# Two fused transformer layers on one core: early weight loads behind the last maxima, another order of the first front, and eight bits before the next maximum

## The chip, the cores and the metric

The kernel runs on one core of a Trainium2 chip. The metric is the device time of one execution in microseconds (us).

## The reference

The input x is (4, 1024, 512) in fp32. Two layers are computed one after the other. The first, "layer 0", is a style-modulated layer norm, an attention with 16 heads of 32 columns, a projection and a second norm:

```python
h = _sln(hidden, w, ...)                      # gamma * ln(hidden) + beta
energy = jnp.einsum('bhqd,bhkd->bhqk', q, k)
att = jax.nn.softmax(energy, axis=-1) / D ** 0.5
h1 = out @ Wp.T + bp + hidden
return _sln(h1, w, ...) + h1
```

The second, "layer 1", does the same kind of attention and a feed-forward block of 2048 columns, with weights of three values and activations of eight bits:

```python
def act_quant(x):
    s = 127.0 / jnp.clip(jnp.max(jnp.abs(x), axis=-1, keepdims=True), EPS)
    return jnp.clip(jnp.round(x * s), -128, 127) / s
xn = adaln(x, c, g1, w_ada1, b_ada1)          # rmsnorm(x) * g * (1 + scale) + shift
x = x + bitlinear(attention(bitlinear(xn, w_qkv, b_qkv)), w_proj, b_proj)
xn = adaln(x, c, g2, w_ada2, b_ada2)
h = jax.nn.gelu(bitlinear(xn, w_fc1, b_fc1), approximate=False)
x = x + bitlinear(h, w_fc2, b_fc2)
```

## The kernel before

The program is written out by hand for the five engines: TensorE (PE), VectorE (DVE), ScalarE (ACT), GpSimd (POOL) and SyncE (SP), which issues the DMAs. Semaphores order them. There are three blocks: `layer0`, `layer1a` (layer 1 up to the attention's projection) and `layer1b` (the feed-forward part). Between two blocks all engines meet.

**Attention.** The class `Attention` serves both layers. One batch has 16 rows (heads). For each row, `max_chunk` (L369) makes 16 chunks of scores whose maxima DVE reduces (L500), two rows ahead of use; these maxima become a row of 8 KB ("row of maxima") that ACT copies out of PSUM (`m_row`, L465) and that SP moves into the last two partitions of q by `load_m` (L295). Only then do the real scores start (`scores`, L383): the first score of a row waits for that transfer. ACT takes the exponential (L461), POOL adds probabilities up three by three (`sums`, L338 and L343), and PE multiplies them with the values and the sums with ones (L401) and folds the result (L408). SP's order is written in `run_sp`: at step k it issues the six pieces of q and k of row k + 3 (`load`, L290), or, at k = 13, when no such row is left, calls `late()`; then it waits for the maxima of row k + 1 and issues `load_m`.

In the last batch of either layer `late()` also holds the loads for the block to come. In `layer0` these are the q/k/v and projection weights of layer 1 (L761, L762). In `layer1a` they are fc1, a quarter of x, the modulation, two biases and fc2 (L1536), six transfers. At k = 13 all of them stand on SP's queue ahead of the `load_m` of rows 14 and 15.

**Fronts.** Ahead of each batch's attention in `layer1a` stands a front: four transposes ("X"), sixteen products of q and k ("QK", each a half of 128 columns) and eight of v ("V"). `products` (L1484 to L1501) writes out their order; the last 14 of them each have two chunks of maxima behind them (a "part", "prelude"). For batch 0 nothing else runs beside the front; for batches 1 to 3 the front is spread over the attention before it and joined with its tail. A QK product is scaled by DVE (L1776), ACT writes its rounded high half (`high`, L1702), and DVE (`low`, L1786; the first eight) or POOL (L1599, after ACT has made the whole value at L1705; the last eight) writes the low half. A V product is scaled by ACT (L1691), and POOL adds the bias (L1582). `load` of row 0 waits for four high and four low halves; ACT's first exponential waits for all sixteen. The value bias lies in memory that the last high half overwrites, so `high` waits for all bias adds at m = KC + 3. The order for batch 0 before is

```python
order = X + both(QK[:EARLY], V) + QK[EARLY:]      # EARLY = 8; both() takes from the two lists in turn
chunks = order[-att.PRELUDE:]                     # PRELUDE = 14
```

and POOL does all eight bias adds, then the eight low halves.

**The last block.** `layer1b` has 32 tiles of 128 tokens. Each engine has a list of stages with offsets; at step n it runs stage f for tile n + offset. For DVE these are the maximum of h (offset 0), the de-quantization of fc1 (`hidden`, L2083, offset 2), the maximum of x (`maximum(0)`, L2050, offset 5), the eight bits of x (`x_bits`, L2074, offset 4), the eight bits of h (`h_bits`, L2089, offset 0) and the residual. PE transposes x (L1950), does fc1 (L1959), transposes h (L1968) and does fc2 (L1978). ACT scales x (L2001), rounds it (L2005), copies transposes (L2009, L2024) and does Gelu. The block opens on ACT with a dummy Sqrt (L1986), the Sqrt of the mean squares (L1988) and a dummy Gelu (L1989), so that the function tables are loaded there.

Of the kernel before, what the change touches and what calls it, by code (L numbers as in the profile page):

```python
# [142 lines left out]
class Attention:  # L143
# [158 lines left out]
    def run_sp(self, sp, b, late, extra=None, ready=None):  # L302
# [4 lines left out]
        def head(i, k, N, ok, steps):  # L307
# [8 lines left out]
            if ok(k + 1):  # L316
                self.load_m(sp, N + 1, (k + 1) % NJ)
        self.loop(b, head)
# [234 lines left out]
def layer0(nc, ins, mod, x_in, x_out, ss1, ident, ps):  # L553
# [4 lines left out]
    with ctx:  # L558
# [141 lines left out]
        with nc.Block() as block:  # L700
            @block.sync
            def _(sp):
# [46 lines left out]
                def batch(b, last):  # L749
                    def late():  # L750
# [7 lines left out]
                        sp.dma_start(bp, rows(ins["bp"], P)).then_inc(s_late, 16)  # L758
                        if last:
                            sp.wait_ge(s_wout, 16 * (2 + done(2) - done(1)))  # L760
                            sp.dma_start(next_w[:, :, :], wq["qkv"]).then_inc(s_next, 16)  # L761
                            sp.dma_start(next_wp[:, :, :], wq["proj"]).then_inc(s_next, 16)  # L762
# [19 lines left out]
                    att.run_sp(sp, b, late, ready=ready)  # L782
# [620 lines left out]
def layer1a(nc, ins, mod, wq, dws, x_in, x_out, ss1, ss2, ident, identb, ps):  # L1403
# [5 lines left out]
    with ctx:  # L1409
# [71 lines left out]
        def products(nxt, tail):  # L1481
# [4 lines left out]
            if not tail:  # L1486
                order = X + both(QK[:EARLY], V) + QK[EARLY:]
# [27 lines left out]
        with nc.Block() as block:  # L1515
            @block.sync
            def _(sp):
# [6 lines left out]
                def attend(b, last):  # L1524
                    def late_load():
                        sp.dma_start(bp, rows(ins["b_proj"], P)).then_inc(s_late, 16)
                        if not last:
                            sp.dma_start(bv, rows(ins["b_v"], P)).then_inc(s_bv, 16)
                            return
                        sp.wait_ge(KINDS["V"][1], TT * B)  # L1530
                        sp.wait_ge(s_store, 16 * TT + 16)
# [11 lines left out]
                    att.run_sp(sp, b, late_load, extra)  # L1543
# [6 lines left out]
                    if not last:  # L1550
                        att.first_loads(sp, b + 1, (2,))

# [19 lines left out]
            def _(pool):  # L1572
# [4 lines left out]
                def work(order, nxt, tail):  # L1577
# [5 lines left out]
                    if nxt is not None:  # L1583
                        biases(range(TT if tail is None else LEAD))
                        if tail is not None:
                            pool.wait_ge(s_q, TT * (tail + 1))
                            biases(range(LEAD, TT))
                    if tail is not None:
                        pool.wait_ge(s_late, 16 * (tail + 1))
                        for t in range(TT):  # L1590
                            if t % 2 == 0:
                                pool.wait_ge(s_res[t // 2], 16 * (tail + 1))
                            pool.tensor_tensor(xres[:, t, :], xres[:, t, :], bp, ALU.add).then_inc(s_xb, 1)
                    if nxt is None:
                        return
                    for v in range(EARLY, UN):
                        pool.wait_ge(s_whole, (UN - EARLY) * nxt + v - EARLY + 1)
                        hi, lo = parts(v)
                        pool.tensor_tensor(lo, qf(v), hi.bitcast(FP32), ALU.subtract).then_inc(s_lo, 1)  # L1599
                pool.sem_inc(s_xb, 1)  # L1600
# [4 lines left out]
            def _(pe):  # L1605
# [46 lines left out]
                def work(order, nxt, tail):  # L1652
                    if nxt is not None and tail is not None:
                        pe.wait_ge(s_qf, UN * nxt + EARLY)
                    for kind, n, bank, before, part in order:
# [3 lines left out]
                        if part is not None:  # L1659
                            if part == 0:  # L1660
# [7 lines left out]
            def _(act):  # L1668
# [24 lines left out]
                def high(n, nxt, tail):  # L1693
# [4 lines left out]
                    if m == KC + 3:  # L1698
                        act.wait_ge(s_val, TT * (nxt + 1))
                        if tail is not None:  # L1700
                            act.wait_ge(s_xb, TT * nxt + 1)
# [142 lines left out]
def layer1b(nc, ins, mod, wq, dws, x_in, out, ss2, identb, ps):  # L1844
# [11 lines left out]
    with ctx:  # L1856
# [23 lines left out]
        one, s_one = sb("one", [P, 2], FP32), sem("one_ok")  # L1880
# [27 lines left out]
        with nc.Block() as block:  # L1908
# [76 lines left out]
            def _(act):  # L1985
                act.activation(one[:, 0:1], identb[:, 0:1], ACT.Sqrt).then_inc(s_one, 1)  # L1986
# [175 lines left out]
```

## Time and profile before

| | |
|---|---|
| median of 3 runs | 2920.75 us (2918.14 to 2922.14) |
| profiled execution, its own time | 2920.18 us |
| its span, first to last instruction | 2918.3 us |
| busy in the span | PE 92%, DVE 76%, POOL 69%, ACT 63%, weight loads 52% |
| mean granted clock of PE | 0.970 |

The profiled execution's time is its span and 1.9 us around it. A line of a timeline has the start in us from the span's start, the duration, the engine, the line of the kernel, the operation, what is written and read, how many instructions are merged, and in square brackets the idle time before and who ended it.

### The profile page before, as it was taken

To read this page: it belongs to the slowest core of one execution; us is meant where nothing else is said; L and a number is where in the kernel's file an instruction comes from. 1 tells how busy PE (TensorE), PEld (TensorE's weight loads), DVE (VectorE), ACT (ScalarE), POOL (GpSimd) and SP (SyncE) were. 2 spreads that over 40 slices of the span, in tenths; PEclk is the share of its full clock that TensorE was granted. 3 is DMA by queue.
4 is the path that set the end of the run, shared out by engine and by line. 5 is a ranking of instruction groups with operands and counts; after the bars stand their busy time and mean duration, and the time that the engine had idled before them with its cause. 6 is when DMAs were issued, how large, how long until landed. Compare 5 with 4: busy or idle time off the path is not lost. (4 is left out here: it accounts for less than half of the span.)

```text
span 2918.3 us, 62297 instructions
## 1 busy us (share of the span) xinstructions
PE 2686.3 (92%) x22313; PEld 1514.9 (52%) x22313; DVE 2216.5 (76%) x4450; ACT 1838.4 (63%) x3314; POOL 2022.7 (69%) x1703
## 2 busy tenths in 40 slices
PE   7899999999999989999669998998999899958998
PEld 6655466554765547555235554554555455424444
DVE  4777678776887768878667768777887777649997
ACT  3366654665566654666346677667666766548887
POOL 0299824996269951899539997997899799854441
PEclk9999999999999999999879999999999999979999
DMA  6122343223432424223123214322232232440000
GB/s 217 39 62 56 123 128 120 56 63 135 138 91 57 128 77 152 70 56 117 51 69 74 60 31 113 81 64 70 74 78 53 62 85 62 144 166 23 29 29 36
DMA packets 102183, 243.57 MB, mean 83 GB/s; under 512 B 18812, under 2 KB 25092, under 8 KB 101000
## 3 DMA queue, kind: packets, MB, share of 16 engines
q1 hardware_dynamic: 100104, 233.49, 28.2%
q0 software_dynamic: 1792, 6.33, 0.6%
q8 instruction: 172, 2.82, 0.4%
q14 instruction: 115, 0.94, 0.1%
HBM read 99.15 MB, written 38.88 MB: 47 GB/s over the span
## 5 line engine op out<-in xcount | busy, mean ns | idle before, releaser
L500 DVE TENSOR_REDUCE a_mxs<-ps 128x1 f32<-128x512 f32 x2048 | 1269.5, 682 | 269.0 <-PE ps L369 266.6
L461 ACT ACTIVATE a_p<-ps 128x512 f32<-128x512 f32 x2048 | 1043.7, 605 | 209.4 <-PE ps L383 200.0
L338 POOL TENSOR_TENSOR a_sum<-a_p 128x512 f32<-128x512 f32 x768 | 989.0, 1294 | 95.8 <-PE ps L401 76.2
L369 PE MATMUL ps<-a_k,a_q 96*128 96x512 f32 x2048 | 858.6, 425 | 34.4 <-DVE a_mxs L500 27.0
L383 PE MATMUL ps<-a_q,a_k 98*128 98x512 f32 x2048 | 812.0, 420 | 23.6 <-ACT a_p L461 11.3
L343 POOL TENSOR_TENSOR a_sum<-a_sum,a_p 128x512 f32<-128x512 f32 x512 | 664.6, 1298 | 40.2
L401 PE MATMUL ps<-a_sum,a_unit 128*32 128x512 f32 x1536 | 657.8, 599 | 17.3 <-POOL a_sum L343 14.6
L401 PE MATMUL ps<-a_p,a_vx 128*32 128x512 f32 x4096 | 665.0, 599 | 1.0 <-DVE tok L519 0.8
L369 PEld LDWEIGHTS ps<-a_k,a_q 96*128 96x128 f32 x2048 | 390.2, 191 | 270.5 <-DVE a_mxs L500 113.0
L383 PEld LDWEIGHTS ps<-a_q,a_k 98*128 98x128 f32 x2048 | 385.0, 189 | 261.5 <-ACT a_p L461 158.9
L470 ACT ACTIVATE a_ots<-ps 128x512 f32<-128x512 f32 x256 | 152.8, 598 | 423.1 <-PE ps L401 422.1
L401 PEld LDWEIGHTS ps<-a_sum,a_unit 128*32 128x32 f32 x1536 | 134.7, 110 | 184.1 <-issue 147.8
L401 PEld LDWEIGHTS ps<-a_p,a_vx 128*32 128x32 f32 x4096 | 166.9, 110 | 109.3 <-issue 74.0
L517 DVE RECIPROCAL a_rec<-ps 128x4 f32<-128x4 f32 x256 | 45.1, 176 | 167.4 <-PE ps L408 167.4
L1934 POOL TENSOR_TENSOR c_tk<-c_tk,b_next_mod 128x512 f32<-128x512 f32 x32 | 40.7, 1271 | 153.7 <-ACT c_tk L2001 153.7
L408 PEld LDWEIGHTS ps<-a_fold,a_ots 128*32 128x32 f32 x8192 | 99.0, 111 | 90.0 <-issue 85.9
L1978 PE MATMUL ps<-b_next_w,c_hT 128*128 128x512 bf16 x512 | 120.5, 379 | 22.1 <-ACT c_hT L2024 22.1
L846 POOL TENSOR_TENSOR kh<-kh,qh 128x512 f32<-128x512 f32 x32 | 43.1, 1346 | 129.1 <-ACT a_p L1080 128.7
L1959 PE MATMUL ps<-b_next_w,c_xqT 128*128 128x512 bf16 x512 | 120.0, 389 | 4.9 <-ACT c_xqT L2009 2.6
L408 PE MATMUL ps<-a_fold,a_ots 128*32 128x33 f32 x8192 | 119.7, 198 | 2.0 <-ACT a_ots L470 2.0
L966 PE MATMUL ps<-qh,ql 128*128 128x512 f32 x256 | 110.8, 593 | 3.3 <-ACT ql L1074 3.3
L1582 POOL TENSOR_TENSOR xv<-xv,kh 128x512 f32<-128x512 f32 x32 | 40.1, 1271 | 81.5 <-ACT xv L1691 81.5
(240 smaller groups left out, 3190.8 us busy)
## 6 DMA issues: line engine op xcount, KB each, us to landing
a_q<-qh SPq DMA_DIRECT2D x256, 128.0 KB, 2.3
a_k<-kh SPq DMA_DIRECT2D x256, 128.0 KB, 2.4
a_q<-ql SPq DMA_DIRECT2D x128, 128.0 KB, 2.4
a_k<-kl SPq DMA_DIRECT2D x128, 128.0 KB, 2.4
x<-a_p SPq DMA_DIRECT2D x64, 256.0 KB, 2.1
a_p<-in_w_fc SPq DMA_DIRECT2D x12, 1024.0 KB, 8.0
kl<-in_x SPq DMA_DIRECT2D x4, 2048.0 KB, 9.5
kh<-in_x SPq DMA_DIRECT2D x4, 2048.0 KB, 14.4
```

The source lines that it names most:

```text
L338: pair = pool.tensor_tensor(tile, self.key_tile(u, kt), self.key_tile(u, kt + 1), ALU.add)
L343: pool.tensor_tensor(tile, tile, self.key_tile(u, kt + 2), ALU.add).then_inc(self.s_sum, 1)
L369: pe.matmul(self.mx[self.mx_ring[at]], self.q[j][0:96, t * P:(t + 1) * P], self.k[j][0:96, half * HALF:(half + 1) * HALF], start=True, sto ...
L383: pe.matmul(self.st[self.st_ring[at]], self.k[j][0:98, kt * P:(kt + 1) * P], self.q[j][0:98, u * HALF:(u + 1) * HALF], start=True, stop=Tr ...
L401: mm = pe.matmul(self.ot[half % 2][HD * c:HD * (c + 1), :], weights, tile, start=r == rounds[0], stop=r == rounds[-1])
L408: mm = pe.matmul(self.ot[u][HD * c:HD * (c + 1), t * (HD + 1):(t + 1) * (HD + 1)], self.ots[:, u, t * P + HD * c:t * P + HD * (c + 1)], se ...
L461: act.activation(self.key_tile(u, kt), self.st[self.st_ring[CHUNKS * k + n]], ACT.Exp, scale=self.scale).then_inc(self.s_exp, 1)
L470: act.activation(self.ots[:, u, :], self.ot[u], ACT.Copy).then_inc(self.s_ots, 1)
L500: dve.reduce_max(self.mxs[:, k % 2, c:c + 1], self.mx[self.mx_ring[CHUNKS * k + c]], axis=AX.X).then_inc(self.s_mxr, 1)
L966: mm = pe.matmul(ps[:, t, :], oT[:, k, t * P:(t + 1) * P], wp[:, k, :], start=k == 0, stop=k == KC - 1)
L1959: mm = pe.matmul(f1[:, j, :], xqT[:, r % 2, k, :], w1[:, k, j * HALF:(j + 1) * HALF], start=k == 0, stop=k == KC - 1)
L1978: mm = pe.matmul(f2, hT[:, r % 2, k, :], w2[:, k, :], start=k == 0, stop=k == FC - 1)
```

## The change

It has five parts. `run_sp` takes a function `after()` and calls it behind the `load_m` of row 15. The loads for the block to come move from `late()` there, in both layers; in `layer1a` x and the modulation now go first, and fc2 goes behind the four residual loads that follow the attention. The order of batch 0's front in `layer1a` has the first eight QK products alone, then V and the last eight QK products in turn; POOL takes bias adds and low halves in turn, and `high` waits for the bias adds at its last call alone. The dummy Sqrt moves from the head of `layer1b` to the head of ACT's last work in `layer1a`. In `layer1b`, DVE's list has `x_bits` ahead of `maximum(0)`.

```diff
@@ Attention.run_sp
             if ok(k + 1):
                 self.load_m(sp, N + 1, (k + 1) % NJ)
+                if not ok(k + 2):
+                    after()
@@ layer0, SP
+                    def after():
                         if last:
                             sp.wait_ge(s_wout, 16 * (2 + done(2) - done(1)))
                             sp.dma_start(next_w[:, :, :], wq["qkv"]).then_inc(s_next, 16)
@@ layer1a, products
-                order = X + both(QK[:EARLY], V) + QK[EARLY:]
+                order = X + QK[:EARLY] + both(V, QK[EARLY:])
@@ layer1a, SP
-                        for dst, src in ((next_w1[:, :, :], wq["fc1"]), (next_x[:, 0:TT, :], x_out[0:T, :].rearrange("(t p) d -> p t d", p=P)),
-                                         (next_mod[:, 0, :, :].rearrange("p i d -> p (i d)"), rows(Pending.mods[2][0, :, :].rearrange("i d -> (i d)"), P)),
-                                         (next_b1[:, :], rows(ins["b_fc1"], P)), (next_b2[:, :], rows(ins["b_fc2"], P)),
-                                         (next_w2[:, :, :], wq["fc2"])):
-                            sp.dma_start(dst, src).then_inc(s_next, 16)
+                    def after():
+                        if last:
+                            sp.wait_ge(KINDS["V"][1], TT * B)
+                            sp.wait_ge(s_store, 16 * TT + 16)
+                            for dst, src in ((next_x[:, 0:TT, :], x_out[0:T, :].rearrange("(t p) d -> p t d", p=P)),
...
+                                             (next_w1[:, :, :], wq["fc1"]), (next_b1[:, :], rows(ins["b_fc1"], P)),
+                                             (next_b2[:, :], rows(ins["b_fc2"], P))):
+                                sp.dma_start(dst, src).then_inc(s_next, 16)
...
                     if not last:
                         att.first_loads(sp, b + 1, (2,))
+                    else:
+                        sp.dma_start(next_w2[:, :, :], wq["fc2"]).then_inc(s_next, 16)
@@ layer1a, POOL
-                        biases(range(TT if tail is None else LEAD))
...
+                    if tail is None:
+                        for t in range(TT):
+                            biases((t,))
+                            rest(EARLY + t)
+                        return
@@ layer1a, PE
-                            if part == 0:
+                            if part == 0 and tail is not None:
                                 pe.wait_ge(s_vs, TT * nxt + EARLY_V)
@@ layer1a, ACT, high
-                    if m == KC + 3:
+                    if n == UN - 2 and tail is not None:
+                        act.wait_ge(s_xb, TT * nxt + 1)
+                    if n == UN - 1:
                         act.wait_ge(s_val, TT * (nxt + 1))
-                        if tail is not None:
-                            act.wait_ge(s_xb, TT * nxt + 1)
@@ layer1a, ACT, work
+                    if nxt is None:
+                        act.wait_ge(att.s_one, 1)
+                        act.activation(att.one[:, :], ident[:, 0:1], ACT.Sqrt).then_inc(att.s_one, 1)
@@ layer1b, ACT
-                act.activation(one[:, 0:1], identb[:, 0:1], ACT.Sqrt).then_inc(s_one, 1)
                 act.wait_ge(s_ms, 1)
                 act.activation(rs[:, :], ms[:, :], ACT.Sqrt).then_inc(s_sd, 1)
@@ layer1b, DVE
-                            (0, factor(1)), (5, maximum(0)), (4, x_bits), (5, clipped(0)), (0, h_bits), (5, inverse(0)),
+                            (0, factor(1)), (4, x_bits), (5, maximum(0)), (5, clipped(0)), (0, h_bits), (5, inverse(0)),
```

## Rows read from the trace of the kernel before

**Rows 1.** Waits of PE over the span: us in total, times, longest us

```profile
PE ps L383 <- DMA a_q<-a_mrow: 8.2, 4, 6.3
```

**Rows 2.** Timeline of SP, last batch of layer 1a

```profile
2515.37 0.38 SPq L1536 DMA_DIRECT2D b_next_w<-wq_fc  x1
...
2528.38 22.08 SPq L295 DMA_DIRECT2D a_q<-a_mrow  x2
```

**Rows 3.** Timeline of PE, last batch of layer 1a

```profile
2531.70 0.50 PE L369 MATMUL ps<-a_k,a_q 96*128 96x512 f32 x1
...
2539.22 0.76 PE L383 MATMUL ps<-a_q,a_k 98*128 98x512 f32 x1 [6.31 <-DMA a_q<-a_mrow]
...
2543.76 0.95 PE L401 MATMUL ps<-a_sum,a_unit 128*32 128x512 f32 x1
```

**Rows 4.** Timeline of PE, last batch of layer 0, the same instructions

```profile
1367.47 0.50 PE L369 MATMUL ps<-a_k,a_q 96*128 96x512 f32 x1
...
1371.29 0.62 PE L401 MATMUL ps<-a_sum,a_unit 128*32 128x512 f32 x1
```

**Rows 5.** Timeline of PE, first front of layer 1a

```profile
1480.79 1.91 PE L1628 MATMUL ps<-a_next_w,b_xqT 128*128 128x512 bf16 x4
...
1497.21 1.19 PE L369 MATMUL ps<-a_k,a_q 96*128 96x512 f32 x2 [6.58 <-issue]
...
1528.14 0.80 PE L383 MATMUL ps<-a_q,a_k 98*128 98x512 f32 x1 [1.72 <-ACT a_p L461]
```

**Rows 6.** Timeline of ACT, last tail of layer 1a and start of layer 1b

```profile
2579.11 5.01 ACT L1675 ACTIVATE tok<-tok,b_am 128x512 f32<-128x512 f32 x8 [5.61 <-DVE b_am L1753]
...
2604.14 1.28 ACT L1986 ACT_TABLE_LOAD   x1 [2.57 <-PEq L110]
...
2605.54 0.21 ACT L1988 ACTIVATE c_rs<-c_ms 128x32 f32<-128x32 f32 x1
...
2616.51 0.71 ACT L2005 ACTIVATE c_tk<-c_tk,c_am 128x512 f32<-128x512 f32 x1
```

**Rows 7.** Waits of PE, last two rows of layer 0 (1361.1 to 1403)

```profile
PE ps L401 <- POOL a_sum L343: 4.2, 3, 1.5
```

**Rows 8.** DMA issues of the page: count, KB each, median us to landing

```profile
b_next_w<-wq_fc SPq DMA_DIRECT2D x2, 2048.0 KB, 13.4
```

**Rows 9.** Timeline of DVE, first front of layer 1a

```profile
1489.94 1.57 DVE L1786 SCALAR_TENSOR_TENSOR kl<-ql,b_bqk,kh 128x512 fp32r<-128x512 f32 x1
...
1503.37 0.74 DVE L1786 SCALAR_TENSOR_TENSOR ql<-qh,b_bqk 128x512 fp32r<-128x512 f32 x1
...
1523.93 0.68 DVE L1776 TENSOR_TENSOR a_p<-ps,b_dqr 128x512 f32<-128x512 f32 x1
1524.52 3.07 DVE L500 TENSOR_REDUCE a_mxs<-ps 128x1 f32<-128x512 f32 x5
```

**Rows 10.** Timeline of SP, first front of layer 1a

```profile
1491.59 1.20 SPq L290 DMA_DIRECT2D a_q<-qh  x2
```

**Rows 11.** Timeline of POOL, first front of layer 1a

```profile
1505.23 1.27 POOL L1582 TENSOR_TENSOR xv<-xv,kh 128x512 f32<-128x512 f32 x1 [3.02 <-ACT xv L1691]
```

**Rows 12.** Busy time by window: us; PE, PEld, DVE, ACT, POOL; clock, DMA share, GB/s

```profile
1497.20:1503.30 6.10, 6.08 (x14) 2.79 (x14) 3.11 (x5) 0.69 (x1) 1.26 (x1) 0.50 0.92 207
1503.40:1526.00 22.60, 18.64 (x73) 8.68 (x73) 22.46 (x42) 14.30 (x21) 11.45 (x9) 1.00 0.10 22
```

**Rows 13.** Timeline of ACT, first exponentials of layer 1a

```profile
1527.49 2.08 ACT L461 ACTIVATE a_p<-ps 128x512 f32<-128x512 f32 x4 [1.37 <-POOL kl L1599]
```

**Rows 14.** Timeline of DVE, start of layer 1b

```profile
2604.18 0.18 DVE L2029 TENSOR_SCALAR c_ms<-ss 128x32 f32<-128x32 f32 x1 [3.37 <-PEq L110]
...
2614.38 0.69 DVE L2050 TENSOR_REDUCE c_am<-c_tk 128x1 f32<-128x512 f32 x1 [2.60 <-POOL c_tk L1938]
2614.98 0.87 DVE L2074 TENSOR_SCALAR c_xq<-c_tk 128x512 bf16<-128x512 f32 x1
```

**Rows 15.** Timeline of DVE, one tile in the loop of layer 1b

```profile
2762.34 1.23 DVE L2089 TENSOR_SCALAR c_hq<-c_h 128x2048 bf16<-128x2048 f32 x1 [0.17 <-ACT c_h L2019]
```

More of the change, by code:

```diff
@@ L300, in first_loads, with run_sp @@
             self.load(sp, b, H * b + j, 0, j)
-    def run_sp(self, sp, b, late, extra=None, ready=None):
+    def run_sp(self, sp, b, late, after, extra=None, ready=None):
         if ready:
@@ L781, in batch @@
                     att.load_m(sp, H * b, 0)
-                    att.run_sp(sp, b, late, ready=ready)
+                    att.run_sp(sp, b, late, after, ready=ready)
                     sp.wait_ge(att.s_pv, att.ROUNDS * H // 2 * (b + 1) + att.PV_CREDIT)
@@ L1542, in extra @@
                             front(b + 1)
-                    att.run_sp(sp, b, late_load, extra)
+                    att.run_sp(sp, b, late_load, after, extra)
                     if not last:
@@ L1582, in biases, with rest @@
                             pool.tensor_tensor(xv[:, t, :], xv[:, t, :], bv, ALU.add).then_inc(s_val, 1)
-                    if nxt is not None:
-                        biases(range(TT if tail is None else LEAD))
-                        if tail is not None:
[L1586 to L1596, printed above, removed]
+                    def rest(v):
                         pool.wait_ge(s_whole, (UN - EARLY) * nxt + v - EARLY + 1)
@@ L1599, in work @@
                         pool.tensor_tensor(lo, qf(v), hi.bitcast(FP32), ALU.subtract).then_inc(s_lo, 1)
+                    if tail is None:
[3 more added lines that the diff above has]
+                        return
+                    if nxt is not None:
+                        biases(range(LEAD))
+                        pool.wait_ge(s_q, TT * (tail + 1))
+                        biases(range(LEAD, TT))
+                    pool.wait_ge(s_late, 16 * (tail + 1))
+                    for t in range(TT):
+                        if t % 2 == 0:
+                            pool.wait_ge(s_res[t // 2], 16 * (tail + 1))
+                        pool.tensor_tensor(xres[:, t, :], xres[:, t, :], bp, ALU.add).then_inc(s_xb, 1)
+                    if nxt is not None:
+                        for v in range(EARLY, UN):
+                            rest(v)
                 pool.sem_inc(s_xb, 1)
@@ L1697, in high @@
                     act.wait_ge(s_qf, UN * nxt + n + 1)
-                    if m == KC + 3:
+                    if n == UN - 2 and tail is not None:
+                        act.wait_ge(s_xb, TT * nxt + 1)
+                    if n == UN - 1:
                         act.wait_ge(s_val, TT * (nxt + 1))
-                        if tail is not None:
-                            act.wait_ge(s_xb, TT * nxt + 1)
                     act.activation(parts(n)[0], qf(n), ACT.Identity, bias=bqk[:, m:m + 1]).then_inc(s_hi, 1)
@@ L1878, in layer1b @@
         col = lambda i, j, n: am[:, i, j, bass.ds(n, 1)]
-        one, s_one = sb("one", [P, 2], FP32), sem("one_ok")
+        one, s_one = sb("one", [P, 1], FP32), sem("one_ok")
         s_wsc = sem("wsc_ok")
@@ L1985, in _ @@
             def _(act):
-                act.activation(one[:, 0:1], identb[:, 0:1], ACT.Sqrt).then_inc(s_one, 1)
                 act.wait_ge(s_ms, 1)
                 act.activation(rs[:, :], ms[:, :], ACT.Sqrt).then_inc(s_sd, 1)
-                act.activation(one[:, 1:2], identb[:, 0:1], ACT.Gelu).then_inc(s_one, 1)
+                act.activation(one[:, :], identb[:, 0:1], ACT.Gelu).then_inc(s_one, 1)
                 act.sem_inc(s_xtc, 1)
```

5 lines of the change are left out of this document (2 added, 3 removed).

## The prediction

> **What bounds the kernel now.** I began with the page's busy times (the table above): TensorE is by far the busiest engine, so time comes back only where it stands still or runs at its lower clock. Next I read whom TensorE waited for [rows 1]. The entry that matters is 8.2 us in four waits for the transfer of the row of maxima, of which 6.3 us are a single one. Then I laid the timelines of all engines side by side around the three places that the diff touches.
>
> **Place 1, the early loads of the last batch of layer 1a.** SP issues the loads for the last block from 2515.37 on, and the 8 KB transfer of row 14's maxima only at 2528.38, behind them [rows 2]. TensorE stands still for 6.31 us until that transfer lands, and the matmuls behind it take until 2543.76 to reach the next group [rows 3]. Layer 0's last batch runs the same rows, and there TensorE doesn't wait at this point [rows 4].
>
> **Place 2, the first front of layer 1a.** TensorE stands still for 6.58 us before the first maxima at 1497.21 and for another 1.72 us behind the first scores, at 1528.14 [rows 5].
>
> **Place 3, the start of the last block.** Its first function table is loaded at 2604.14 with nothing else to do [rows 6].
>
> **Part by part.**
>
> *Loads behind the last row of maxima, layer 1a.* From the L369 matmul ahead of row 14's scores to the next L401 group takes 2543.76 - 2531.70 = 12.06 us [rows 3]; the same stretch in layer 0 takes 1371.29 - 1367.47 = 3.82 us [rows 4]. Without the queue the difference goes: **8.2 us**, the wait and the slower restart behind it together. At the upper end I put 8.5. The lower end is set by POOL's sums: in layer 0's last two rows TensorE waits 4.2 us for them [rows 7], and a TensorE that is no longer held up might meet that wait here, which leaves 4.0. I take 8.2, since in layer 0 VectorE adds a bias beside POOL in those rows and in layer 1a it doesn't. The moved loads hang on a wait of SP that both kernels satisfy long before. SP issues x, the modulation, fc1 and two biases after row 15's transfer, near 2542 (2528.38 + 22.08 [rows 2] - 8.2), and fc2 behind four residual loads, before the tail's first rounding, which is now at 2579.11 [rows 6], so by 2571. The transfers of fc1 and fc2 took 13.4 us to land [rows 8], so the last lands by 2584, ahead of the block that reads them, which opens near 2596 (2604.14 - 8.2). Behind them on SP stand only the output stores, which follow the tail. Cost: nothing, as long as those 12 us are there.
>
> *The same in layer 0.* TensorE shows no wait at that transfer [rows 4], so **0**. The bound from both sides is 0.3 us, the spacing of one score. The two weights move by some 20 us and are read 100 us later.
>
> *The order of the first front.* Row 0's pieces of q and k are loaded when four products have their high and low halves. The fourth low half starts at 1489.94 and takes 1.57 us [rows 9]; SP issues the first load at 1491.59 [rows 10]; TensorE's first maxima follow at 1497.21 [rows 5]. In the new order no value product stands between the first eight q/k products, and no value bias runs on POOL yet, so I take 0.74 us for a low half (the row at 1503.37, where POOL stands still: its next add, at 1505.23, follows 3.02 us of idling [rows 11]) instead of 1.57. The second product, now a q/k one, ends at 1480.79 + 1.91 = 1482.70 [rows 5]. Behind it VectorE has four scalings, 0.59 apart (1523.93 to 1524.52), and four low halves, 0.66 apart (1503.37 to the next row) [rows 9]: 1482.8 + 2.4 + 2.7 = 1487.9. Loads and first maxima are **3.6 us** earlier. The other gain lies behind them. Now all eight low halves and nine scalings precede the first maxima, where five low halves and six scalings did: 3 x 0.66 + 3 x 0.59 = **3.8 us** of VectorE work leave the stretch behind, in which VectorE sets the pace: from 1503.4 to 1526.0 it is busy 22.46 of 22.60 us, with TensorE at a granted clock of 1.00 and busy 18.64 [rows 12]. Against this stands a new wait. The last high half must not overwrite the value bias before POOL's eighth bias add, and POOL now does that add only after the seventh "rest"; each takes 1.27 us [rows 11]. Counting ACT's and POOL's queues from the last two products, the high half starts 1.0 to 1.1 us later than its scaling allows. ACT's exponentials wait for POOL's last rest (1527.49) [rows 13], and TensorE behind them (1528.14). Queued behind the waiting high half are only its own second half and the exponentials, so that is the whole price. Sum 3.6 + 3.8 - 1.0 = **6.4 us**. Lower end 3.6 (the loads alone); upper end 7.4, without POOL's part. In the joint rounds, where one batch's tail runs with the next one's front, the two high halves wait for the same POOL adds as before, in POOL's order: 0.
>
> *The Sqrt table.* The load (1.28 us) and its dummy go to the head of ACT's last work in layer 1a, where ACT stands still for 5.61 us [rows 6]: free there. If that cover were gone it would cost 1.5. In the last block the Sqrt starts at 2605.54; its input leaves VectorE at 2604.18 + 0.18 [rows 6, 14], so it can start near 2604.45: **1.1 us**. Ends: 0, and 1.4, the whole distance from 2604.14. The Trainium skill ("ScalarE: Activation LUTs", What ACT_TABLE_LOAD costs) puts a switch at about 1.28 us for the load and 1.38 us more to drain, so by it the sum would come to 18.1 and the time to 2902.1; the trace doesn't agree, for the Sqrt starts 0.12 us behind the load's end with the dummy in between.
>
> *Eight bits ahead of the next maximum.* Tile 0's eight bits came behind the maximum of tile 1, for which VectorE had stood idle 2.60 us until 2614.38; they ran at 2614.98 for 0.87 us [rows 14]. This looks like 2.6 us, but isn't: ACT copies tile 0's transposes only behind the rounding of tile 1 (2616.51) [rows 6], which needs tile 1's own maximum. With the eight bits out of the way, clip and inverse follow the maximum directly, and the rounding starts near 2615.5: **1.0 us**. Ends: 0 and 2.6. In the steady loop the maximum's result no longer has the eight bits as cover before its clip, yet the next operation, the eight bits of h, already waits 0.17 us for ACT there [rows 15]: cost 0. Ends: no gain, since TensorE's transposes of x aren't what it waits for there, and the loss of rival 4; I stay near the first, as only the latency of one result is exposed.
>
> **Sum:** 8.2 + 6.4 + 1.1 + 1.0 = 16.7 us, off the profiled execution's 2920.2: 2903.5. That execution lies 0.6 below the median of the runs, 2920.75; I give **2904.0**.
>
> **Rivals.**
> 1. *POOL takes over from the transfer.* The four-microsecond wait of layer 0 [rows 7] appears in layer 1a too: the first term is 4.0, the sum 12.5, the time 2908. For it: the last rows end on POOL sums in both layers. Against: VectorE's bias adds are absent. 10%.
> 2. *The prelude stays at TensorE's lower clock.* After the stop TensorE's granted clock is 0.50 (1.2 of 2.4 GHz) for 6.1 us, in which it does 14 matmuls [rows 12]; a part has six (four of a product, two of maxima), so it takes 2.6 us there. The later ones are paced by VectorE, with two reductions of 0.61 (3.07 / 5 [rows 9]) and every second time a scaling: 1.5 us. Were the last eleven slow too, 11 x 1.1 = 12.1 us would come back: the sum is 4.6, the time 2916. Against: TensorE will stand still for about 2.7 instead of 6.58 us. 7%.
> 3. *The table load comes back.* The last block opens with a load of its own, so that term is 0 and the sum 15.6: 2905. The Trainium skill ("ScalarE activation tables: per-element evaluation and per-set limits", Table sets in the compiler and the runtime) says that the table loads are placed per block. The trace leaves it open: in it every change of block is also a change of table. 8%.
> 4. *VectorE becomes the bound of the last block.* In each of 32 tiles the maximum (0.69 us [rows 14]) is no longer covered and h's eight bits come that much later: 32 x 0.69 = 22.1 us lost, the sum is -5.4, the time 2926, slower than before. It decides from the point where the clip comes more than the 0.17 us of slack late in every tile and TensorE's transposes of h wait for it. Against: only a result's latency is exposed, not the maximum. 4%.
> 5. *The change does nothing in place 1*, because the transfer itself was slow and not the loads ahead of it: 2912. Only four of these transfers were waited for at all, the other three for 1.9 us together [rows 1], so I put this within the rest.
>
> **How the numbers follow.** Forecast 68%, rivals 10, 7, 8 and 4%, rest 3%. About 0.2% (5.8 us) is what a measurement of this kernel can tell from no change. The forecast, rivals 1 to 3 and a third of the rest are faster: 94%. Rival 4 lies at the edge between same and slower, so I split it and what is left of the rest: 4% same, 2% slower. The range goes down to 2898, where the upper ends of all terms lie (8.5 + 7.4 + 1.4 + 2.6 = 19.9) with 2 us to spare for a clock that rises earlier, and up to 2911, which holds rival 1 and any one term at its lower end. Rivals 2, 4 and 5 stay outside.
>
> **What would show it.** TensorE's wait on the maxima's transfer without the 6.3 us; the first load of row 0 near 1488 and the first exponential near 1521 instead of 1527.5; no table load between the two layers' blocks except that of Gelu, and the first fc1 matmul some 2 us sooner after the block's start; an unchanged period of a tile in the loop. Wrong would be: a POOL wait of over 3 us in layer 1a's last two rows, products 1.7 us apart until the prelude's end, or a longer tile period.

## The result, and the profile after

The changed kernel took 2897.76 us in the median of 4 runs (2896.73 to 2900.11), the kernel before beside it 2919.44 (2917.23 to 2922.14): a ratio of 0.9926, interval 0.9909 to 0.9944, or 21.7 us less. The forecast was 2904.0, so the direction is right and the median lies 0.24 us under the range's low end. Two further comparisons of the same two kernels, told below, give 17.3 and 17.5 us. The profiled execution took 2898.03 us with a span of 2896.3.

Lines of the changed kernel stand 2 to 17 lower in the file than those of before. TensorE's waits over the whole span, the row that answers to [rows 1]:

```profile
PE ps L385 <- DMA a_q<-a_mrow: 2.8, 4, 1.3
```

The 6.3 us wait is gone. In place 1, SP now issues row 14's and row 15's transfers ahead of every load (timelines of SP and of TensorE, last batch of layer 1a, for [rows 2] and [rows 3]):

```profile
2515.86 13.50 SPq L295 DMA_DIRECT2D a_q<-a_mrow  x2
2529.47 0.40 SPq L1543 DMA_DIRECT2D b_next_x<-x  x1
```

```profile
2519.19 0.50 PE L371 MATMUL ps<-a_k,a_q 96*128 96x512 f32 x1
2519.53 0.40 PE L385 MATMUL ps<-a_q,a_k 98*128 98x512 f32 x1
...
2523.01 0.62 PE L403 MATMUL ps<-a_sum,a_unit 128*32 128x512 f32 x1
...
2549.40 1.03 PE L403 MATMUL ps<-a_sum,a_unit 128*32 128x512 f32 x1 [1.51 <-POOL a_sum L345]
...
2550.22 1.06 PE L403 MATMUL ps<-a_sum,a_unit 128*32 128x512 f32 x1
```

The stretch of 12.06 us is 2523.01 - 2519.19 = 3.82 us, to the hundredth what layer 0 had [rows 4]. But at the attention's end the groups behind the wait for POOL follow each other 0.82 us apart (2549.40 to 2550.22), where they stood 0.43 us apart until then: the granted clock is 0.50 from 2549.40 to 2552.00, so TensorE runs at 1.2 GHz there.

The first front, for [rows 5, 9 to 13]: SP, TensorE, VectorE, POOL and ACT in turn.

```profile
1482.04 1.20 SPq L290 DMA_DIRECT2D a_q<-qh  x2
```

```profile
1487.62 1.22 PE L371 MATMUL ps<-a_k,a_q 96*128 96x512 f32 x2 [2.69 <-DMA a_k<-kh]
...
1515.99 0.80 PE L385 MATMUL ps<-a_q,a_k 98*128 98x512 f32 x1 [2.26 <-ACT a_p L463]
```

```profile
1481.23 0.74 DVE L1803 SCALAR_TENSOR_TENSOR kl<-ql,b_bqk,kh 128x512 fp32r<-128x512 f32 x1
...
1490.61 0.69 DVE L1793 TENSOR_TENSOR a_p<-ps,b_dqr 128x512 f32<-128x512 f32 x1 [0.87 <-PE ps L1642]
1491.22 1.28 DVE L502 TENSOR_REDUCE a_mxs<-ps 128x1 f32<-128x512 f32 x2
1493.62 1.29 DVE L502 TENSOR_REDUCE a_mxs<-ps 128x1 f32<-128x512 f32 x2 [1.12 <-PE ps L371]
```

```profile
1511.13 1.26 POOL L1591 TENSOR_TENSOR xv<-xv,kh 128x512 f32<-128x512 f32 x1
1514.04 1.26 POOL L1596 TENSOR_TENSOR kl<-a_p,kh 128x512 fp32r<-128x512 f32 x1 [1.65 <-ACT a_p L1719]
```

```profile
1512.48 0.73 ACT L1716 ACTIVATE kh<-a_p,b_bqk 128x512 fp32r<-128x512 f32 x1 [1.94 <-POOL xv L1591]
...
1515.34 2.08 ACT L463 ACTIVATE a_p<-ps 128x512 f32<-128x512 f32 x4 [1.37 <-POOL kl L1596]
```

The first load starts 0.07 us behind the fourth low half (1481.23 + 0.74), and the low halves take 0.74 us as forecast. The new wait of the last high half for POOL's bias is there, 1.94 us long. This execution is 6.0 us ahead when layer 0 ends (see below); with these set back, the first load lies at 1488.05 and the first exponential at 1521.35, where 1488 and 1521 were forecast. In the windows view (columns as in [rows 12]) the first maxima run at 1.2 GHz, after that VectorE again sets the pace:

```profile
1487.60:1493.80 6.20, 5.93 (x13) 2.79 (x14) 3.35 (x6) 2.89 (x5) 3.90 (x4) 0.50 0.92 204
1493.80:1512.00 18.20, 16.54 (x67) 7.75 (x67) 17.95 (x34) 10.34 (x17) 13.74 (x12) 0.99 0.06 14
```

Place 3, for [rows 6, 14, 15]: ACT, then VectorE at the last block's start and in its loop.

```profile
2553.38 1.28 ACT L1725 ACT_TABLE_LOAD   x1
2554.67 0.20 ACT L1725 ACTIVATE a_one<-ident 128x1 f32<-128x1 f32 x1
...
2585.86 0.23 ACT L2004 ACTIVATE c_rs<-c_ms 128x32 f32<-128x32 f32 x1 [2.76 <-DVE c_ms L2045]
2586.11 1.28 ACT L2005 ACT_TABLE_LOAD   x1
```

```profile
2585.64 0.18 DVE L2045 TENSOR_SCALAR c_ms<-ss 128x32 f32<-128x32 f32 x1 [3.30 <-PEq L110]
...
2592.79 0.83 DVE L2090 TENSOR_SCALAR c_xq<-c_tk 128x512 bf16<-128x512 f32 x1 [0.68 <-ACT c_tk L2021]
2594.78 0.69 DVE L2066 TENSOR_REDUCE c_am<-c_tk 128x1 f32<-128x512 f32 x1 [1.16 <-POOL c_tk L1955]
...
2634.10 0.15 DVE L2073 TENSOR_SCALAR c_am<-c_am  x1 [0.15 <-DVE c_am L2066]
2634.18 1.23 DVE L2105 TENSOR_SCALAR c_hq<-c_h 128x2048 bf16<-128x2048 f32 x1
```

The Sqrt stands 0.22 us behind its input's start (1.36 before), with no load of its own; the only load left in the block is Gelu's. Tile 0's bits come 2 us ahead of tile 1's maximum. In the loop only a result's latency of 0.15 us is exposed, and the eight bits of h no longer wait.

**Where the 22 us lie.** I took the start of ACT's copy of each row of maxima (line 465 before, 467 after) as a mark in both traces and subtracted. The changed kernel is ahead by 1.1 us at the first mark, and by 6.0 us at the last one of layer 0 (1376.77 against 1370.76), where the change has done nothing yet but hold back loads in layer 0's last rows. Layer 1a's first front adds 6.3, place 1 adds 8.6 (21.09 at the last mark of layer 1a), the rest of layer 1a loses 2.6, and the last block's start gains 3.2 again. So the change's own steps make about 16 us of this pair, and 6 us came from somewhere else. Of these, 1.1 stand at the first mark, some 1.4 in layer 0's front ahead of its second batch and 3.3 in the one ahead of its fourth. What follows asks from where.

### The profile page after: what moved, and what is told of

Read it like the earlier page. It is cut to its first block and busy times, and to the rows that moved or that the text cites. A ratio compares the mean times of both kernels' runs of the same rounds, so it can differ in the third digit from the quotient of the medians.

```text
span 2896.3 us, 62255 instructions
## 1 busy us (share of the span) xinstructions
PE 2671.8 (92%) x22259; PEld 1509.2 (52%) x22313; DVE 2214.3 (76%) x4450; ACT 1836.7 (63%) x3314; POOL 2020.8 (70%) x1703
```

## The experiments

Each kernel was timed beside the kernel before. Besides the times I read the same stretches from each kernel's one profiled execution, as differences of starts in its timelines; they tell single steps apart better than a median. **L0** is a front of layer 0, from row 15's mark of its third batch to row 0's of the fourth; **front** goes from layer 0's last mark to layer 1a's mark of row 1; **place 1** from its mark of row 14 to that of row 15 in the last batch; **end** from there to VectorE's last write of the attention's result; **tail** to c_ms, the mean squares that VectorE writes first in the last block; **block** to the first fc2 matmul. All in us.

| kernel | L0 | front | place 1 | end | tail | block |
|---|---|---|---|---|---|---|
| before | 138.96 | 157.82 | 21.46 | 24.74 | 29.88 | 38.21 |
| e1, loads alone | 135.49 | 157.92 | 12.87 | 25.78 | 31.53 | 37.76 |
| e2, front alone | 135.61 | 149.36 | 20.90 | 24.76 | 30.25 | 37.75 |
| e3, block alone | 135.87 | 159.40 | 21.25 | 24.66 | 31.07 | 34.92 |
| e4, layer 0 alone | 137.09 | 159.31 | 21.32 | 24.68 | 30.36 | 38.03 |
| after | 135.69 | 151.51 | 12.88 | 25.69 | 31.48 | 34.98 |
| e5, the same | 137.22 | 150.36 | 12.86 | 25.73 | 31.48 | 35.01 |
| e14, the same | 138.66 | 149.42 | 12.88 | 24.71 | 30.06 | 35.53 |
| e6, without block | 135.68 | 149.35 | 12.88 | 24.66 | 31.37 | 37.71 |
| e8, idle products | 138.70 | 149.34 | 12.89 | 24.68 | 30.44 | 34.15 |
| e9, V first | 135.91 | 148.40 | 12.88 | 25.70 | 31.45 | 35.01 |
| e12, before + idle | 138.86 | 158.01 | 21.38 | 24.70 | 29.73 | 36.03 |
| e11, e1 + idle | 135.91 | 159.33 | 12.89 | 25.72 | 29.93 | 36.01 |
| e10, e8 + e9 | 135.68 | 148.79 | 12.88 | 24.70 | 30.48 | 32.50 |
| e13, e10 + front idle | 135.74 | 148.31 | 12.87 | 25.75 | 30.19 | 32.50 |

### The parts alone

**e1**, layer 1a's loads behind the last row of maxima, layer 0 in its old order:

```diff
-                    att.run_sp(sp, b, late, ready=ready)
+                    att.run_sp(sp, b, late, lambda: None, ready=ready)
...
-                    att.run_sp(sp, b, late_load, extra)
+                    att.run_sp(sp, b, late_load, after, extra)
```

> Only the loads of the last block are moved behind the last row of maxima (layer 1a; layer 0 keeps its order). My theory (the parts add up as the steps of the prediction say; the 6 us by which the changed kernel is ahead in layer 0's fronts is how the clock fell in that execution, not the change): the first product over a row of maxima goes from 2531.70 us to some 8.4 us earlier, the end of the attention and the tail give back 2.5 us as in the changed kernel's trace (products at the lower clock), so 5.5 to 6.5 us faster in all, and layer 0's fronts end within 2 us of the kernel before. Rival A (giving back belongs to the other parts): 8.2 to 8.6 us faster. Rival B (this part also speeds up layer 0): 12 us faster, with layer 0's last row of maxima 5 us or more earlier.

2911.60 against 2918.10 us, ratio 0.9978 (0.9969 to 0.9987): 6.5 us, with an interval of 3.8 to 9.0 us that holds rival A as well. The stretches decide: place 1 gives 8.6, and end and tail give back 1.0 and 1.6, as my theory has it. That the tail's share belongs to this part is not shown, though: e3, without it, has a tail 1.2 us longer than before's. And layer 0's last mark stands at 1373.06, 3.7 us ahead of the kernel before, where the theory had it within 2: a miss, taken up under e4.

**e2**, the first front alone:

```diff
-                order = X + both(QK[:EARLY], V) + QK[EARLY:]
+                order = X + QK[:EARLY] + both(V, QK[EARLY:])
```

> Only the first front of layer 1a has its new order (eight q and k in front, the V products between the later ones, biases and rests in turns, the waits of the later halves). My theory: 6.3 us faster, of which all stands at layer 1a's first row of products and none ahead of it; layer 0's fronts as before. Rival A (the front's gain is lost again by the end): under 3 us. Rival B (layer 0 is sped up by this part): 12 us.

2910.73 against 2918.10, 0.9975 (0.9965 to 0.9984): 7.4 us. The front itself is 8.5 us shorter than in the trace of before, 2 more than forecast; the last part of this document says where these 2 lie.

**e3**, the Sqrt's table and x_bits:

```diff
+                        act.activation(att.one[:, :], ident[:, 0:1], ACT.Sqrt).then_inc(att.s_one, 1)
...
-                            (0, factor(1)), (5, maximum(0)), (4, x_bits), (5, clipped(0)), (0, h_bits), (5, inverse(0)),
+                            (0, factor(1)), (4, x_bits), (5, maximum(0)), (5, clipped(0)), (0, h_bits), (5, inverse(0)),
```

> Only the last block's two edits: the Sqrt's table is loaded in the tail of layer 1a, and x_bits stands ahead of the next tile's maximum. My theory: 1.1 us for the table and 0.9 us for x_bits, 2 us faster; up to 1.2 us more if the products of the block's start go back to the full clock earlier as in the changed kernel's trace, so 2 to 3.3 us. Rival A (these go into a wait behind the block's start): 0 to 0.5 us. Rival B (layer 0 is sped up too): 8 us.

2915.66 against 2918.10, 0.9993 (0.9984 to 1.0002): 2.4 us, which by itself can't be told from no change; the block's start is 3.3 us shorter than before and some 2.9 shorter than in e1, e2 and e4.

**e4**, layer 0's loads alone:

```diff
-                    att.run_sp(sp, b, late, ready=ready)
+                    att.run_sp(sp, b, late, after, ready=ready)
```

> Only layer 0's loads for layer 1a stand behind its last row of maxima. My theory: no change, within 0.6 us (nobody waits for that row of maxima in layer 0), and the fronts of layer 0, which this code doesn't touch, as in the kernel before, within the 2 us by which executions differ. Rival (the code of layer 0 as the change leaves it runs its fronts faster): 5 to 6 us faster, there ahead of layer 0's last batch.

2918.67 against 2918.10, 1.0002 (0.9993 to 1.0011): nothing. Yet its profiled execution ends layer 0 at 1372.20, 4.6 us ahead of the trace of before. So do e1, e2 and e3 (1373.06, 1372.44, 1373.58), with old code there. The 2 us by which my theories let executions differ were too few, and the 6 us are not the change's.

**What the 6 us are.** The windows of that front of layer 0 and of 24 us at its start (columns as in [rows 12]), in the kernel before and in the changed one:

```profile
1027.00:1166.00 139.00, 127.34 (x685) 83.24 (x685) 102.01 (x198) 69.48 (x116) 46.26 (x36) 0.95 0.37 119
1040.00:1064.00 24.00, 19.00 (x186) 10.61 (x183) 4.79 (x12) 10.68 (x19) 11.39 (x10) 0.79 0.36 119
```

```profile
1027.00:1166.00 139.00, 128.49 (x671) 84.85 (x664) 105.14 (x202) 68.59 (x112) 44.09 (x36) 0.98 0.38 123
1040.00:1064.00 24.00, 19.89 (x193) 10.17 (x193) 9.92 (x23) 9.25 (x17) 8.76 (x7) 1.00 0.52 175
```

The mean granted clock is 0.79 in the one and 1.00 in the other. The third run of the changed kernel, e14, has a row like that of before, and its L0 is 138.66:

```profile
1040.00:1064.00 24.00, 19.30 (x182) 10.54 (x182) 6.28 (x16) 9.33 (x17) 9.96 (x8) 0.79 0.43 155
```

This front's code is the same in all fifteen traces. Over these 24 us the clock is 0.79 in four of them (before, e8, e12, e14), with an L0 of 138.7 to 139.0, and 1.00 in the other eleven, with 135.5 to 137.2. So one and the same code takes some 3 us more where TensorE's clock is lower; what makes it fall there in some executions is open.

### The whole again

**e5** and, in a later comparison, **e14**: the changed kernel with no edit.

> The changed kernel itself, in more runs beside the kernel before. Theory A (the parts only add up; 4 of the 22 us of the first comparison came from how layer 0's fronts fell in few executions): the sum of the four parts as measured (6.5 + 7.4 + 2.4 - 0.6 = 15.7 us), so a ratio of 0.9940 to 0.9950 against the kernel before. Rival B (the parts strengthen each other): 0.9924 to 0.9932, 20 us or more faster, with the profile showing where the further 4 us are.

> The changed kernel once more beside the kernel before. Theory A (the sum of the parts, 15.7 us alone and 17.3 us in the second comparison, is the change's worth; the 21.7 us of the first comparison is how the clock fell in four executions): ratio 0.9937 to 0.9950. Rival B (the change is worth the 21.7 us, and the second comparison drew low): 0.9920 to 0.9930.

e5: 2902.48 against 2919.79, 0.9943 (0.9929 to 0.9957), 17.3 us. e14: 2901.18 against 2918.70, 0.9945 (0.9931 to 0.9959), 17.5 us. Theory A both times: the parts add up (6.5 + 7.4 + 2.4 - 0.6 = 15.7), and the interval of the 21.7, 16.3 to 26.6 us, holds both. Whether those four executions fell low by chance or, for instance, by the chip they ran on, no run decides.

**e6**, the changed kernel with e3's edits undone:

> The changed kernel without its two edits of the last block (the Sqrt's table is loaded at the block's start again, x_bits stands behind the next maximum). Alone these two edits measured 2.4 us. Theory A (parts add up): 2 to 3 us slower than the changed kernel beside it. Rival B (the parts strengthen each other at the block's start: the products go back to the full clock earlier only when both the loads and these edits are there): 4 to 6 us slower.

2903.95, 0.9950 (0.9936 to 0.9963), 1.5 us over e5 beside it. Nearest to theory A, a little under it, and the two intervals overlap; the block's start is 2.7 us longer than in e5, the end 1.1 shorter.

### What is given back

**e8**, idle products in TensorE's waits of the tail and the block's start:

```diff
+                        pe.matmul(ps[:, 5, :], identb, wp[:, i % KC, :], start=True, stop=True)
...
+                        pe.matmul(ps[:, 5, :], identb, w1[:, i % KC, 0:HALF], start=True, stop=True)
```

> The changed kernel with idle products added (identity by a loaded weight tile into a bank that nobody reads): 14 ahead of the tail's first transpose, 2 ahead of each of the next five, 3 ahead of the projection, 20 at the start of the last block and 8 behind its first transposes. Theory A (what is given back behind the last attention is TensorE at 1.2 GHz after its waits in the tail): the granted clock is 1.00 in the projection and in the block's first fc1, the projection takes 7.0 us rather than 8.25 and fc1 of the first tile 3.6 rather than 5.0, 2 to 3 us faster than the changed kernel. Rival B (the clock falls all the same, or the added products delay the useful ones): same within 0.5 us or up to 2 us slower, with the projection at 8 us or more.

2896.48, 0.9921 (0.9907 to 0.9935), 6.0 us under e5 beside it. The granted clock from the attention's end to the block's start was 0.84 against 0.68 (windows, e8 and then the changed kernel):

```profile
2554.00:2586.00 32.00, 20.65 (x122) 9.11 (x109) 20.13 (x35) 16.58 (x32) 11.04 (x8) 0.84 0.55 198
```

```profile
2553.40:2585.60 32.20, 13.55 (x95) 7.11 (x96) 19.11 (x32) 16.02 (x30) 10.73 (x8) 0.68 0.51 196
```

The first fc1 takes 3.63 us, not 5.02 (timelines of TensorE, e8 and then the changed kernel):

```profile
2596.44 3.63 PE L1986 MATMUL ps<-b_next_w,c_xqT 128*128 128x512 bf16 x16 [1.35 <-ACT c_xqT L2043]
```

```profile
2597.15 5.02 PE L1976 MATMUL ps<-b_next_w,c_xqT 128*128 128x512 bf16 x15 [2.86 <-ACT c_xqT L2025]
```

By stretches this is worth 1.0 in the tail and 0.9 in the block. The end, 1.0 shorter, lies ahead of the first idle product and isn't theirs. So of the 6.0 us some 2 are shown to be the clock kept up in the places named. The rest is not shown: the two profiled executions differ by 1.6 us only (2898.08 and 2896.48), and of the others there is no trace.

**e12** and **e11** put the same products into the kernel before and into e1.

> The kernel before with the idle products of the warm run in the tail and at the last block's start, and nothing else. It stands beside the next kernel, to price the early loads where TensorE keeps its clock. Theory A (the products of the tail and the block's start cost 2 us at the lower clock in this kernel too): 1.5 to 3 us faster than the kernel before. Rival: same within 0.5 us.

> The early loads of the last block alone (as in the first experiment, where they were worth 6.5 us although the product over the last row of maxima came 8.6 us earlier), with the same idle products. Theory A (what was given back is TensorE's lower clock in the tail): 7.5 to 8.6 us faster than the kernel before with the idle products alone, and the stretch from the attention's end to the block's start 30.0 to 30.5 us in both. Rival B (what was given back lies elsewhere): again 6 to 7 us faster than that kernel, with that stretch longer by 1 us or more.

e12: 2915.67 against 2918.21, 0.9993 (0.9984 to 1.0002), 2.5 us, which by itself can't be told from no change. e11: 2909.58, 0.9968 (0.9958 to 0.9978), 6.1 us under e12, where 7.5 to 8.6 were expected: a miss in the totals, as rival B has it. The stretches say more. The tail is 29.93 and 29.73 us, so the 1.6 us lost in e1's tail are gone but for 0.2, which is theory A; the end keeps its 1.0 us (25.72 and 24.70), which no idle product covers; and e11's first front took 1.3 us longer than e12's with the same code, for its block began 3.2 us later behind layer 0's last mark. Between medians an effect of 1 us can't be told.

### Toward a faster kernel

**e9**, the V products one place earlier:

```diff
-                order = X + QK[:EARLY] + both(V, QK[EARLY:])
+                order = X + QK[:EARLY] + V[:1] + both(V[1:], QK[EARLY:-1]) + QK[-1:]
```

> The changed kernel with the V products one place earlier in the first front (V0 ahead of the ninth q or k, the last q or k alone at the end) and GpSimd's bias of a tile ahead of the rest of the half before it, so that ScalarE's last high half no longer waits for the last bias (1.94 us in the changed kernel's profile). Theory A (that wait is on the path to the first exponential): the first exponential starts 1.0 to 1.3 us earlier (1514.1 instead of 1515.34 in the profile's time), the kernel 1 us faster. Rival B (the row of maxima's transfer or VectorE's last maxima set the end): within 0.3 us of the changed kernel. Rival C (a V product ahead of the first later q delays VectorE): 0.5 to 1 us slower.

2897.60, 0.9925 (0.9912 to 0.9939), 4.9 us under e5 beside it. The last high half now waits 0.32 us, for VectorE, and no longer for POOL (timeline of ACT):

```profile
1511.99 0.72 ACT L1718 ACTIVATE kh<-a_p,b_bqk 128x512 fp32r<-128x512 f32 x1 [0.32 <-DVE a_p L1795]
...
1514.85 3.09 ACT L463 ACTIVATE a_p<-ps 128x512 f32<-128x512 f32 x6 [1.37 <-POOL kl L1596]
```

From layer 0's last mark the first exponential stands at 142.33 us, against 143.05 to 143.14 in e2, e6, e8 and e14: 0.7 to 0.8 us, and the front is 1.0 us shorter. That is theory A, the exponential short of its 1.0 to 1.3, since VectorE's scaling now holds up the high half. The rest of the 4.9 us is not shown: the profiled executions of e5 and e9 differ by 1.6 us.

**e10** joins e8 and e9; **e13** adds idle work ahead of the first front:

```diff
+                        for i in range(50):
+                            pe.transpose(ps[:, 5, 0:P], ident, ident)
...
+                                    pe.matmul(ps[:, 7, :], identb, w[:, i % KC, 0:HALF], start=True, stop=True)
```

> The changed kernel with both additions: the V products one place earlier in the first front, and the idle products. If both gains stand by themselves: 4 us faster than the changed kernel in the same sense as before (0.9925 of the kernel before for the V products, 0.9921 for the idle products, 0.9943 for the changed kernel), so 0.990 to 0.9915 of the kernel before. Rival (the two gains were mostly how the clock fell in layer 0): 0.992 to 0.9935.

> The same with more idle products ahead of layer 1a's first front: 50 and 12 transposes of the identity around the last scales of layer 0 and 6 products ahead of the first maxima of layer 1a. Theory A (the first maxima of that front, which run at 1.2 GHz until 1493.8 us in the changed kernel's profile and leave VectorE idle for 0.87 and 1.12 us between them, are bound by TensorE's clock): that stretch at the full clock, 1.5 to 2.5 us faster than the kernel without them. Rival B (the transfers of the first q and k, or VectorE, bind the front, or the clock falls all the same): within 0.7 us. Rival C (the idle work delays layer 0's end): 1 us or more slower.

e10: 2894.73 against 2918.21, 0.9923 (0.9909 to 0.9937), in the rival's range: the two gains over e5 don't add up. That the clock in layer 0 made part of them, as the rival has it, is not shown. e13: 2894.10, 0.9920 (0.9906 to 0.9933), 0.6 us less, rival B by the number. The clock did rise as theory A wants it: 1.00 in the stretch with the first maxima, against 0.84 in e10 (windows, e13 and then e10):

```profile
1486.00:1497.00 11.00, 9.19 (x39) 4.55 (x40) 9.24 (x16) 6.66 (x11) 8.68 (x7) 1.00 0.70 156
```

```profile
1486.00:1497.00 11.00, 9.30 (x33) 4.46 (x34) 8.27 (x14) 6.07 (x10) 7.70 (x6) 0.84 0.73 162
```

Row 0's maxima leave 1.0 us earlier, and so does the first exponential, but the mark of row 1 only 0.5. From the first exponential to that mark (windows, e13 and then e10) the clock is lower again, and VectorE, busy for 4.5 of 6.9 us, is not what binds:

```profile
1511.80:1518.70 6.90, 6.26 (x17) 4.89 (x18) 4.49 (x12) 5.41 (x10) 5.82 (x6) 0.56 0.03 6
```

```profile
1513.20:1519.70 6.50, 5.83 (x16) 4.31 (x17) 4.63 (x12) 5.36 (x11) 5.42 (x6) 0.63 0.04 9
```

So half of what the idle work gained was paid again at the lower clock right behind it. The medians of both kernels lie below the changed one, which stood at 0.9943 and 0.9945 in its two longer comparisons, but the intervals overlap.

## Why the prediction was right, and where it failed

**Loads of layer 1a, -8.2: right, with a debt left out.** Place 1 gave 8.5 to 8.6 in all kernels with them. Forecast at nothing, though, was what comes behind: end and tail were 1.0 and 1.6 us longer in e1, so 5.9 arrive at the last block, whose start is 0.5 shorter; the medians give 6.5. The end was 1.0 us longer in six of the ten traces with the early loads (25.7 to 25.8 us) and in none of the five without (24.7); in the changed kernel its last groups ran at 1.2 GHz. The tail's share is mostly the projection (timelines of TensorE: e1; e3, without the early loads; e14, with them):

```profile
2582.39 8.33 PE L1635 MATMUL ps<-a_next_wp,tok 128*128 128x512 bf16 x31 [1.77 <-ACT tok L1690]
```

```profile
2591.67 8.13 PE L1628 MATMUL ps<-a_next_wp,tok 128*128 128x512 bf16 x31 [1.77 <-ACT tok L1683]
```

```profile
2574.65 6.85 PE L1642 MATMUL ps<-a_next_wp,tok 128*128 128x512 bf16 x31 [1.61 <-ACT tok L1697]
```

It takes 8.1 to 8.7 us where its granted clock is 0.81 to 0.84, and 6.9 to 7.1 where that is 1.00, as in all traces with idle products. Without them it is slow in five of six traces with the early loads, and in one of four without. So the clock is the price, but that the early loads bring it on is likely and not shown, and why it falls is open. The prediction's time for the moved loads, near 2542, leaves out that the shorter front brings them forward too (2529.47, or 2535.5 with the 6.0 us of layer 0 set back); nothing hangs on it. Rival 1 falls: POOL's wait in the last rows is 1.5 us, as before.

**Layer 0's loads, 0: right** (e4).

**First front, -6.4: right in mechanism; the clock came on top.** Five kernels with the new order have 149.3 to 150.4, against 157.82 in the trace the sum was made from: 7.5 to 8.5 us; only the profiled execution of the first comparison shows 6.3. Counted from layer 0's last mark, the first load comes at 114.82 before, 111.28 after and 111.18 in e2 (3.5 to 3.6 earlier, as forecast). From the first maxima to row 0's mark (windows: before, after, e2):

```profile
1497.20:1522.40 25.20, 22.23 (x77) 10.01 (x78) 22.07 (x40) 11.93 (x17) 10.17 (x8) 0.88 0.26 58
```

```profile
1487.60:1509.70 22.10, 21.37 (x75) 10.07 (x78) 19.00 (x35) 12.38 (x19) 15.54 (x13) 0.85 0.30 66
```

```profile
1489.20:1509.90 20.70, 20.16 (x75) 9.56 (x78) 18.85 (x35) 12.25 (x19) 15.52 (x13) 0.92 0.32 70
```

VectorE has 3.1 to 3.2 us less to do here, not 3.8: the three low halves and three scalings are gone as counted, but 25 reductions stand ahead of the mark where 24 did. The changed kernel's maxima run at 1.2 GHz for the first 6 us as before, and its stretch is 3.1 shorter. The new wait then costs 0.6, not 1.0. So the first exponential comes 6.1 earlier and row 1's mark 6.3, where 6.4 was forecast: the two errors nearly cancel, which is luck. In e2 the clock is back after 3.4 us, and the stretch is 4.5 shorter. From the first exponential to row 1's mark another 0.8 comes back there, again with the clock (windows: before, e2):

```profile
1527.50:1534.60 7.10, 6.46 (x17) 4.93 (x18) 4.64 (x12) 5.45 (x11) 6.02 (x6) 0.53 0.11 24
```

```profile
1515.50:1521.80 6.30, 5.62 (x18) 4.23 (x18) 4.20 (x11) 5.30 (x10) 5.22 (x5) 0.73 0.05 10
```

e14, the changed kernel itself, has e2's times (149.42 in all), so some 2 us of this front go with the clock and differ between executions of one program. Rival 2 holds for the first 3 to 6 us of maxima only (clock 0.50, then 0.99).

**Sqrt table, -1.1: right**, 1.36 to 0.22. Rival 3 falls: the Sqrt ran in the last block on the table loaded in the block before. The Trainium skill ("ScalarE activation tables: per-element evaluation and per-set limits", Table sets in the compiler and the runtime) says that the back end places the table loads per block; in this trace no load of Sqrt's table stands in the last block. The 1.38 us of draining that the Trainium skill adds to a load ("ScalarE: Activation LUTs", What ACT_TABLE_LOAD costs) don't show either: at 2553.38 the load takes 1.28 and the next activation starts 0.01 us behind it.

**x_bits, -1.0: right in size; the loop, 0: right.** From c_ms to the first fc1 matmul it is 2597.15 - 2585.64 = 11.51 against 13.57 (2617.75 before), so 2.06 for both edits, forecast 2.1. The clock behind it rises earlier: the first tile's fc1 takes 5.02 us, where before it took 6.18, which brings the block to 3.2 in this pair and to some 2.9 in e3 against e1, e2 and e4.

```profile
2617.75 6.18 PE L1959 MATMUL ps<-b_next_w,c_xqT 128*128 128x512 bf16 x16 [1.24 <-ACT c_xqT L2009]
```

Rival 4 falls: the first fc2 matmuls follow each other 8.87 us apart in the loop of both kernels. Rival 5 falls with place 1.

**The step that failed is the range's low end**, and under it what the sum takes over unchanged from one execution: TensorE's clock, and with it all code that the change leaves alone. The end was put where "the upper ends of all terms lie", "with 2 us to spare for a clock that rises earlier". The runs showed that the same code differs by more than these 2 us. In the profiled pair layer 0 was 6.0 us ahead though nothing that changed there mattered (e4), 3.3 of them in the front whose clock was 1.00 and not 0.79; its last mark lies anywhere from 1370.4 to 1376.8 us in the fifteen traces, and the sum rested on the latest of them. The first front of one program differs by 2 us with the clock, so that the front's term, sized at 6.4 with an upper end of 7.4, measured up to 8.5; and the tail's projection differs by 1.3 to 1.6.

Of the 6.2 us from 2904.0 to 2897.76, 1.3 come from the kernel before, which took 2919.44 beside it and not 2920.75; for the other 4.9 the profiled pair points to layer 0, as the change's own steps make 16 us there, against a sum of 16.7. The other three executions left no trace, so for them the cause stays open. That the sum is so near the 17.3 and 17.5 of the longer comparisons (2902.48 and 2901.18, inside the range) is in part luck: the clock's 2 us in the front and a debt of up to 2.6 us, both left out, nearly cancel.

## What to carry to other kernels

A small transfer on which a matmul waits goes ahead of large loads on its queue; the gain can be read beforehand from the same stretch in a place without the loads. Then look at what TensorE does next: a gain can be paid again in part at the lower clock behind it, and idle products in the waits brought that back in the tail and the block's start here. Before a difference of a few microseconds is explained, subtract the traces at marks and see whether it arises where the change is.

## What was not expected of the hardware

The front of layer 0 called L0 took 135.5 to 139.0 us in fifteen executions of the same code, with a granted clock of 0.79 or 1.00 over the same 24 us. And idle work can pay: 55 products that nobody reads made the block's start of the kernel before 2.2 us shorter (38.21 to 36.03); its median came out 2.5 us lower, which by itself can't be told from no change.
